# Attention kernel: the value products of two key tiles made in one visit to the column-tiled products

## The reference

```python
# x: (2, 2048, 512), H = 16 heads, DH = 32 columns a head, float32
q = (x @ wq_w + wq_b).reshape(b, s, H, DH).transpose(0, 2, 1, 3)
k = jnp.einsum('bsl,hld->bhsd', k_lat, upk_w) + upk_b[None, :, None, :]
v = jnp.einsum('bsl,hld->bhsd', v_lat, upv_w) + upv_b[None, :, None, :]
scores = jnp.einsum('bhqd,bhkd->bhqk', q, k) / jnp.sqrt(jnp.float32(DH))
scores = jnp.where(causal[None, None], scores, -jnp.inf)
attn = jax.nn.softmax(scores, axis=-1)
out = jnp.einsum('bhqk,bhkd->bhqd', attn, v)
```

## Time and profile before

| | |
|---|---|
| median of three runs | 2580.83 us |
| the profiled execution | 2585.65 us |
| its span, first to last instruction | 2584.1 us |
| TensorE busy | 2359.1 us (91%) |
| VectorE busy | 1520.0 us (59%) |
| ScalarE busy | 1045.7 us (40%) |
| GpSimd busy | 1124.1 us (44%) |
| mean granted TensorE clock | 0.945 of full speed |

### The profile page before, as it was taken

The page is one execution under the profiler, slowest core; times in us unless marked ns, Lnnn a source line. Parts: engine busy times, 40 slices in busy tenths (PEclk is TensorE's granted clock), DMA queues, the critical chain, the costliest instruction groups (busy, mean ns, idle before and its releaser), DMA issues. The chain is left out here.

```text
span 2584.1 us, 33911 instructions
## 1 busy us (share of the span) xinstructions
PE 2359.1 (91%) x12216; PEld 1507.0 (58%) x12216; DVE 1520.0 (59%) x3164; ACT 1045.7 (40%) x1928; POOL 1124.1 (44%) x689
## 2 busy tenths in 40 slices
PE   5998499999999999999999869999678999999997
PEld 5776244444444444444444247777577887878786
DVE  2665686767777676767677154444454555555553
ACT  2332045555555555555555622221103333333332
POOL 0000046555666656565565743131023444454543
PEclk8999599999999999999999979999858999999999
DMA  3766611314131231513130024342134655666561
GB/s 102 267 230 248 142 34 34 82 34 99 30 87 34 51 82 45 142 34 83 30 81 10 27 88 145 114 146 82 51 100 133 195 192 188 202 195 200 181 165 33
DMA packets 167008, 285.34 MB, mean 110 GB/s; under 512 B 25934, under 2 KB 68046, under 8 KB 166864
## 3 DMA queue, kind: packets, MB, share of 16 engines
q1 hardware_dynamic: 142608, 210.04, 27.2%
q0 software_dynamic: 24256, 73.43, 9.5%
HBM read 198.60 MB, written 91.88 MB: 112 GB/s over the span
## 5 line engine op out<-in xcount | busy, mean ns | idle before, releaser
L840 ACT ACTIVATE b_pt<-b_st 128x512 f32<-128x512 f32 (+3 forms) x1280 | 613.0, 535 | 492.2 <-DVE b_st L802 205.0
L657 POOL TENSOR_TENSOR b_acc<-b_acc,b_pt 128x1024 f32<-128x1024 f32 (+1 forms) x256 | 592.7, 2346 | 219.4 <-ACT b_pt L840 219.1
L781 DVE TENSOR_REDUCE b_mpart<-b_mx 128x1 f32<-128x512 f32 x768 | 512.2, 686 | 203.0 <-PE b_mx L897 200.4
L918 PE MATMUL b_st<-b_q,b_k 97*128 97x512 f32 (+2 forms) x1280 | 498.5, 402 | 74.3 <-ACT b_pt L840 54.8
L897 PE MATMUL b_mx<-b_k,b_q 96*128 96x512 f32 (+2 forms) x1280 | 510.3, 414 | 29.8 <-DVE b_mt L789 25.9
L897 PEld LDWEIGHTS b_mx<-b_k,b_q 96*128 96x128 f32 x1280 | 249.2, 196 | 286.6 <-DVE b_mpart L781 154.4
L918 PEld LDWEIGHTS b_st<-b_q,b_k 97*128 97x128 f32 x1280 | 242.9, 191 | 280.9 <-ACT b_pt L840 239.9
L931 PE MATMUL b_ob<-b_pt,b_v 128*32 128x512 f32 (+3 forms) x2560 | 304.0, 547 | 1.1 <-ACT b_pt L840 1.1
L778 DVE CUSTOM_DVE_ANT_0 b_unread<-b_mx,b_later 128x384 bf16<-128x384 f32 (+3 forms) x512 | 244.6, 484 | 89.4 <-PE b_mx L897 89.1
L657 POOL TENSOR_TENSOR b_acc<-b_pt 128x1024 f32<-128x1024 f32 x48 | 113.4, 2378 | 299.1 <-ACT b_pt L840 299.1
L61 PE MATMUL e_fb<-e_xh,e_w_guh 128*128 128x512 f32 (+1 forms) x552 | 220.9, 400 | 1.5 <-DVE e_xl L1759 1.5
(11 more groups left out here) (233 smaller groups left out, 3545.8 us busy)
## 6 DMA issues: line engine op xcount, KB each, us to landing
b_q<-scr_qh SPq DMA_DIRECT2D x64, 256.0 KB, 4.4
b_k<-scr_kh SPq DMA_DIRECT2D x64, 256.0 KB, 4.0
e_gu<-in_L_ffn_w_gate_dram SPq DMA_DIRECT2D x23, 704.0 KB, 4.4
e_gu<-in_L_ffn_w_up_dram SPq DMA_DIRECT2D x23, 704.0 KB, 5.9
e_d<-in_L_ffn_w_down_dram SPq DMA_DIRECT2D x23, 512.0 KB, 7.0
a_xin<-in_L_attn_x_dram POOLq DMA_DIRECT2D x8, 1024.0 KB, 5.8
scr_qh<-a_qh SPq DMA_DIRECT2D x8, 1024.0 KB, 4.5
scr_ql<-a_ql SPq DMA_DIRECT2D x8, 1024.0 KB, 6.7
```

What stands on the lines that cost most here:

```text
L657: g.tensor_tensor(out[:, :, lo:], so_far[:, :, lo:], pt[n % NPB][:, :, lo:], ALU.add).then_inc(s_add, 1)
L781: v.tensor_reduce(part, mxb[i % NMX][:, 0:w], AX.X, ALU.max).then_inc(s_red, 1)
L840: act.activation(pt[n % NPB][:, j, lo:], stb[:, (2 * n + j) % NST, lo:], ACT.Exp, scale=SCALE).then_inc(s_exp, 1)
L918: pe.matmul(stb[:, (2 * n + j) % NST, lo:], kb[:, h, at:at + P], qb[:, h, q * CH + lo:(q + 1) * CH], start=True, stop=True).then_inc(s_st, 1)
```

## The change

Value products are no longer made in every odd step, but in every second odd step, from step 5 on, and there for two key tiles in a row. The products of the later of the two tiles stay in the step where they were; those of the earlier one come two steps later than they did. The last two pairs follow the loop.

```diff
                     if n % 2 == 0 and n >= 4:
                         count_ones((n - 4) // 2)
-                    if n % 2 and n >= 3:
+                    if n % 4 == 1 and n >= 5:
+                        values((n - 5) // 2)
                         values((n - 3) // 2)
                     for i in range(some[0], some[1]):
                         item(i)
@@
                         finish(done)
+                values(NS // 2 - 2)
                 values(NS // 2 - 1)
                 count_ones(NS // 2 - 2)
                 count_ones(NS // 2 - 1)
```

## The result

The changed kernel takes 2638.72 us in the median of four runs (2626.03 to 2644.71), the one before 2580.63 with a fourth run added to its three. The ratio is 1.0223, with a 95% interval of 1.0180 to 1.0267: **58 us slower**. The forecast was slower, by 12 us, in a range up to 2618. The sign was right and the size was not.

What follows compares the result with a forecast made beforehand. TensorE's stream was taken to set the attention's pace. Moved columns' 13.8 us minus net gains at vacated places gave 1.6 us a head group, +13 over eight, taken as +12 on 2580.83: 2593 us, range 2552 to 2618.

Steps and rivals of the forecast that it cites:

- Masked sites: Ten of twenty vacated places a head group, where the step before masks: removing the visits gives 3.6 us.
- unmasked ones: The other ten vacated places a head group, with no mask beside them: removing the visits gives 9.0 us.
- the readers ran dry: ScalarE and VectorE, already idle behind a single visit, would idle some 0.8 us more behind a double one.
- TensorE's busy time was to fall by 45 us: Sign in the attention's middle stretch: TensorE's busy time falls by about 45 us while the stretch gets no shorter.
- 13.8 - (3.6 + 9.0 - 0.4) = 1.6 us a head group, times 8: Moved columns' cost minus gains at the vacated places, less ring waits: +13 us over eight head groups, taken as +12.
- Over the twenty sites 1.7 us are absorbed: New places in a head group: existing waits absorb 1.7 of the moved columns' 15.5 us, leaving 13.8.
- I take 0.4 us a head group: Steps beyond the one after a vacated place: full maxima buffers cost 0.4 us, bounds 0 and 2.
- The first group is bound by maxima and the last has none, both at about nothing either way: First and last head groups: the change costs or gains about nothing, so +12 us was taken instead of +13.
- The drain is all that counts: Rival: buffers absorb the uneven order, middle stretch keeps 46 us of saved drain, 2534 us; faster cases together 0.31.
- It cancels: Rival: gains and costs of moving the value products cancel to within 8 us; chance 0.25.
- The readers become the bound: Rival: between double visits with eight or more maxima and no sum visit, up to +48 us, 2629; chance 0.10.
- the saved 53 us: Entry and drain removed from TensorE by joining visits: 160 times 0.33 us.

Runs made afterwards that it cites:

- e1: Kernel before, joining only the 80 value-product pairs whose vacated step has no diagonal tile: 2584.8 us against 2574.0, ratio 1.0047.
- e2: Kernel before, joining only the 80 value-product pairs whose vacated step has a diagonal tile: 2652.64 us, ratio 1.0299 to the kernel before.
- e7: Changed kernel plus three zero products in each of 72 vacated steps under diagonal tiles: 2615.48 us, ratio 1.0155 to the kernel before.
- e11: Kernel before plus three zero products in even steps behind a diagonal tile without a sum visit: 2575.0 us against 2579.68, ratio 0.9987.
- e4: Changed kernel without the diagonal tiles' masks: 2498.97 us, against 2505.11 for the kernel before without masks.
- e6: Kernel before with 88 joins in the other phase, odd pairs delayed where the vacated step has no diagonal tile: 2572.53 us against 2576.36, ratio 0.9988.

## Why the prediction was right and wrong

**Right: the sign and its mechanism.** The prediction said that what counts is what the time at the old place was covering. Masked sites gave 3.15 us a head group (forecast 3.6), unmasked ones 9.2 (9.0), and without masks the ten masked sites give 10.2. e1 against e2 shows that the masked joins carry the loss. At the same step the readers ran dry by 0.9 us more behind a double visit (forecast 0.8), and it lasted 1.85 us (1.83). One sign failed: TensorE's busy time was to fall by 45 us in the middle stretch. It rose by 6 at the lower clock, and at full clock it fell by 2.3 us in the second head group (136.5 to 134.3), some 18 for eight.

**The step that failed: "13.8 - (3.6 + 9.0 - 0.4) = 1.6 us a head group, times 8", with no term beside it for the clock.** At full clock a head group cost 3.7 us; between the two filled kernels, e7 and e11, five of the six middle ones cost 3.8 to 4.0. "Over the twenty sites 1.7 us are absorbed" was 0.9: the joined steps cost 14.6 us, not 13.8. "I take 0.4 us a head group" for the steps behind was 1.4, and 1.3 of it lies in even steps that mask themselves, where I had looked for maxima filling their ring. These two are 1.8 us; with the 0.3 that the old places gave less it is 2.1 a head group, 17 us in all.

**Put at nothing without a reason: the clock.** No term of the sum and no rival had it, though the earlier trace rows show 0.87 in the stretch from 1384.6, where TensorE waits most. The second head group keeps its full clock and costs 3.7 us; the fourth and fifth, the same steps with drops, cost 9.8 and 9.7. The experiments put the clock at 15 to 18 us of the 58.

**Also set at nothing: "The first group is bound by maxima and the last has none, both at about nothing either way."** Units 0 to 3 grew from 173.0 to 179.8 us and the last unit from 52.1 to 56.5, where the like unit of the second head group grew by 1.9. That is 3.1 and 2.5 us beyond the rate of the second head group. With both kernels filled (e7 against e11) units 0 to 3 differ by 5.9 us and the last unit by 4.6, so most of it isn't clock. In the last unit it isn't the masks either: its vacated steps on diagonal tiles give about what they give in the second head group, while its joined steps cost 8.5 us instead of 6.8, and there TensorE waits for exps. What makes the difference was not isolated.

Adding up: 30 us of waits in eight head groups at the second one's rate (8 x 3.7), about 6 more at the ends and 15 to 18 of clock make 51 to 54. The medians differ by 58, the attentions of the two profiles by 52, and the pieces come from single profiles, so they can't be held to a microsecond.

**The rivals.** "The drain is all that counts" was wrong even without masks: e4 kept 6 us of 53, by medians whose intervals overlap. "It cancels" describes e6, and nearly e1. "The readers become the bound" came out near its size, but by another mechanism; its price has a slip: 48 us beyond my sum is 2641, and 2629 is 48 beyond the kernel before. Its place was to be runs of maxima without a sum visit; the runs show masks, and e4 leaves no more than the saved 53 us to be eaten that way. The rule of the Trainium skill, TensorEngine Tiling (Array Packing), "PSUM Bottleneck", that PSUM's readers are the next limit, may describe the taker of the gain in e4, and not the loss. The one of the same page, "Key Properties", on mode switches agrees with the trace: the double visit holds TensorE for 1.85 us and has no gap.

**Left open.** Why one head group keeps its full clock and the next, in the same order of steps, doesn't. What the first and the last head group lose beyond the others. And where e1's 0.5% lies.

## What to carry to other kernels

Before moving work away from where it stands, ask what latency it covers there: taking away a block of products beside a chain of two other engines gives back its full length only if the chain is shorter than what remains. The chain includes what stands ahead of it in its engines' queues, here two reductions ahead of the mask. Count a saved switch last. Where a wait on TensorE can't be removed, cheap products that add nothing may pay by keeping its clock (0.7% in e7, 0.1% and not clear of zero in e11), and better still is to choose which blocks to join so that no vacated place lies beside such a chain.

## What the hardware showed that was not expected

TensorE's granted clock drops in the middle of a stream that is over 80% busy. Two windows of the changed kernel at one drop, in the fourth head group:

```profile
808.40:818.80 10.40, 8.72 (x51) 4.23 (x48) 6.97 (x18) 4.61 (x12) 8.31 (x4) 1.00 0.00 0
818.80:825.60 6.80, 6.80 (x35) 3.46 (x35) 2.94 (x6) 2.38 (x6) 0.00 (x0) 0.50 0.49 118
```

After 10.4 us at 84% busy, with mask waits in between, it runs for 6.8 us at 1.2 GHz with no idle time at all. This drop and one of 3.4 us from 859.7 lie in the unit shown above: with them it takes 49.1 us, and its like at full clock 44.7. The loads of the stretch (DMA share 0.49) aren't the cause by themselves: e7 has a share of 0.60 at the same place, 817.5 to 824.3, at clock 1.00.

Three zero products a place, 0.7 us in steps where TensorE had stood idle for 0.1 to 1.5 us, brought the time at 1.2 GHz in e7's middle stretch from 67 to 7 us. In the kernel before they took it from 20 to none, and a unit from 48.0 to 43.7 us.
